# A bank that ScalarE seeds: the first of seven products is copied into the accumulator of the fourth, and VectorE's sum of the two goes

## The reference, cut to what matters

```python
def _L0_ffn_ref(hidden_states, w_gate, w_up, w_down):
    def _bitlinear(x, w):
        scale = jnp.mean(jnp.abs(w))
        q = jnp.round(jnp.clip(w / (scale + EPS), -1.0, 1.0))
        return x @ (q * scale).T
    gate = _bitlinear(hidden_states, w_gate)   # w_gate (2752, 1024)
    up = _bitlinear(hidden_states, w_up)       # w_up   (2752, 1024)
    return _bitlinear(gate * up, w_down)       # w_down (1024, 2752)
x = x + _L0_ffn_ref(_L0_cond_ref(x, cond, ...), w_gate, w_up, w_down)   # x (64, 64, 1024)
```

## Time and profile before

| | |
|---|---|
| median of 3 runs | 1727.45 us (1727.34 to 1729.59) |
| profiled execution, first to last instruction | 1726.1 us; the page gives no other time of it |
| what lies around the span, median less span | 1.35 us |
| TensorE matmuls, busy | 1707.7 us, 12424 instructions |
| VectorE, busy | 1096.0 us, 1786 instructions |
| ScalarE, busy | 575.6 us, 921 instructions |
| granted TensorE clock, mean | 0.999 |

### The profile page before, as it was taken

How to read it: one execution, slowest core, us unless ns; L and a number is a source line. 1 busy time by engine, 2 the same in 40 slices (tenths; PEclk the granted TensorE clock), 3 DMA queues, 4 the chain that set the end, 5 groups by cost and what they waited for, 6 DMA issues and landing times.

```text
span 1726.1 us, 31355 instructions
## 1 busy us (share of the span) xinstructions
PE 1707.7 (99%) x12424; PEld 1215.6 (70%) x12424; DVE 1096.0 (63%) x1786; ACT 575.6 (33%) x921; POOL 28.0 (2%) x59
## 2 busy tenths in 40 slices
PE   6999999999999999999999999999999999999999
PEld 5554545968769596795958768596776959678684
DVE  6898895555766468554685646755576545855464
ACT  6887732312333133230333213231233313323120
POOL 0010000000000000000000000000000000000000
PEclk9999999999999999999999999999999999999999
DMA  8666626312242032420224211331223313132021
GB/s 342 249 229 239 221 96 219 121 44 97 76 148 96 22 108 77 168 66 22 107 102 164 65 75 54 129 137 43 97 76 126 101 40 108 65 124 79 29 87 49
DMA packets 59735, 194.06 MB, mean 112 GB/s; under 512 B 5280, under 2 KB 5600, under 8 KB 59584
## 3 DMA queue, kind: packets, MB, share of 16 engines
q1 hardware_dynamic: 56432, 177.49, 28.9%
q0 software_dynamic: 2560, 14.36, 2.2%
q10 hardware_dynamic: 592, 0.09, 0.0%
HBM read 160.90 MB, written 31.01 MB: 111 GB/s over the span
## 4 chain that ended last, share of the span: by engine, by line
PE 97%; DVE 2%; DMA 1%; issue 0%; ACT 0%; SPq 0%; DVEq 0%
PE ps L881 52%; PE ps L938 25%; PE ps L658 17%; PE ps L899 2%; PE ps L761 1%; DMA xa<-in_x_dram 1%; DVE wsum L1318 0%; DVE ys L1413 0%; DVE msk L1458 0%; DVE ys L1380 0%; DVE xa L1529 0%; DVE prod L1496 0%; DVE yp L1418 0%; ACT wdT L1106 0%; SPq L493 0%
## 5 line engine op out<-in xcount | busy, mean ns | idle before, releaser
L881 PE MATMUL ps<-yp,wgT 128*128 128x256 f16 x4116 | 902.4, 273 | 1.1 <-issue 1.1
L881 PE MATMUL ps<-wuT,wgT 128*128 128x256 f16 x4116 | 902.4, 273 | 0.0
L881 PEld LDWEIGHTS ps<-yp,wgT 128*128 128x128 fp8e4 x4116 | 402.9, 98 | 50.8 <-issue 2.9
L881 PEld LDWEIGHTS ps<-wuT,wgT 128*128 128x128 fp8e4 x4116 | 402.7, 98 | 48.3
L938 PE MATMUL ps<-wdT,inter 128*128 128x512 fp8e4 x1960 | 433.2, 379 | 0.0
L938 PEld LDWEIGHTS ps<-wdT,inter 128*128 128x128 f16 x1960 | 191.1, 98 | 227.2 <-issue 1.4
L1762 DVE SCALAR_TENSOR_TENSOR xr<-ps,osc,xr 128x512 f32<-128x512 f32 x210 | 156.4, 748 | 168.2 <-PE ps L938 128.4
L1711 DVE TENSOR_TENSOR wdT<-ps,msk 128x512 f32<-128x512 f32 (+1 forms) x77 | 51.3, 666 | 207.1 <-PE ps L881 207.1
L1241 ACT COPY raw<-ps 128x512 f32<-128x512 f32 (+1 forms) x77 | 43.7, 567 | 314.6 <-PE ps L881 314.0
L1248 ACT COPY msk<-ps 128x512 f32<-128x512 f32 (+1 forms) x77 | 43.6, 567 | 138.1 <-PE ps L881 138.1
L1263 ACT COPY inter<-ps 128x256 f32<-128x256 f32 x70 | 26.1, 372 | 180.1 <-PE ps L881 180.1
(11 more groups left out here) (229 smaller groups left out, 1497.9 us busy)
## 6 DMA issues: line engine op xcount, KB each, us to landing
wgT<-wcomb SPq DMA_DIRECT2D x70, 896.0 KB, 4.7
wdT<-dcomb SPq DMA_DIRECT2D x14, 2240.0 KB, 10.9
xa<-in_x_dram SPq DMA_DIRECT2D x8, 2048.0 KB, 7.8
out_dram<-xr SPq DMA_DIRECT2D x64, 256.0 KB, 2.0
wcomb<-xa POOLq DMA_DIRECT2D x17, 448.0 KB, 3.0
xr<-in_L_ffn_w_down_dram SPq DMA_DIRECT2D x9, 512.0 KB, 5.5
inter<-in_L_ffn_w_gate_dram SPq DMA_DIRECT2D x7, 512.0 KB, 16.6
wdT<-in_L_ffn_w_up_dram SPq DMA_DIRECT2D x7, 512.0 KB, 4.4
```

Of the source, the lines that this page charges most:

```text
L881: last = nc.tensor.matmul(out, w, operand(i, OPERAND[what])[:, k, :], start=(start and h + k + i == 0), stop=(k == KQ - 1 and i == 1), ski ...
```

## The change

P2 gets no first-matmul flag any more: ScalarE's `copy_p1` copies P1 from `PB` straight into `PA` (ps4), and P2 accumulates on it, so that `PA` holds P1 + P2. VectorE's `c11` is gone. A new ScalarE copy, `gate11`, brings the gate half of `PA` to SBUF (`g11`, half of the old `t1`), and `i11` takes its up half from PSUM. P2 now waits for `s_t1`, and `copy_p1` for `s_i11` of the pair before (pairs 0 and 6: for the outputs that still read ps4). TensorE's order is P1, P4 of the pair before, P2; in pair 0, which has no P4 before it, the first half of P5 (8 matmuls) stands between P1 and P2, and its second half stays where P5 was.

```diff
-                first, start = isinstance(c, int) and c == FIRST, what in ("P1", "P2", "P5")
+                first, start = isinstance(c, int) and c == FIRST, what in ("P1", "P5")
...
-                elif what == "P2":
-                    if p == 0:
-                        pe.wait_ge(s_o, done - 1)
...
-                    else:
-                        pe.wait_ge(s_c11, n)
-                elif what == "P6":
+                elif what in ("P2", "P6"):
                     pe.wait_ge(s_t1, n + 1)
...
                     product(c, p, "P1")
-                    product(c, p, "P2")
                     if p:
                         product(c, p - 1, "P4")
+                    else:
+                        product(c, p, "P5", 0)
+                    product(c, p, "P2")
                     if more and p - 2 in range(KH):
                         conv(c + 1, p - 2)
                     product(c, p, "P6")
-                    product(c, p, "P5")
+                    product(c, p, "P5", None if p else 1)
...
             def copy_p1(c, p):
                 n, w = NS * (c - FIRST) + p, width(p)
                 act.wait_ge(s_m1, n + 1)
...
+                    act.wait_ge(s_i11, NPR * (c - FIRST) + p)
+                nc.scalar.copy(PA[:, 0:w], PB[p % 2][:, 0:w]).then_inc(s_t1, 1)
+
+            def gate11(c, p):
+                act.wait_ge(s_m2, NS * (c - FIRST) + p + 1)
+                if p == NPR:
+                    act.wait_ge(s_i21, NS * (c - FIRST) + NPR)
+                elif p:
+                    act.wait_ge(s_i11, NPR * (c - FIRST) + p)
+                nc.scalar.copy(g11 if p < NPR else g21, PA[:, 0:HALF]).then_inc(s_g11, 1)
...
                     if p:
                         gate21(c, p - 1)
+                    gate11(c, p)
                     copy_p16(c, p)
...
-                V.tensor_tensor(rr if p < NPR else g21, PA[:, 0:w], t1[:, 0:w], ALU.add).then_inc(s_c11, 1)
-
             def i11(c, p):
-                dve.wait_ge(s_c11, NS * (c - FIRST) + p + 1)
+                dve.wait_ge(s_g11, NS * (c - FIRST) + p + 1)
...
-                V.scalar_tensor_tensor(a_block(p, A11), rr[:, u], PROD, rr[:, g], ALU.mult, ALU.mult).then_inc(s_i11, 1)
+                V.scalar_tensor_tensor(a_block(p, A11), PA[:, u], PROD, g11, ALU.mult, ALU.mult).then_inc(s_i11, 1)
```

More of the change, by code:

```diff
@@ L347, in quarter @@
             return ys[:, k:k + KQ, t:t + HALF]
-        t1, q67 = (raw5[:, i * TOK:(i + 1) * TOK] for i in range(2))
+        g11, q67 = raw5[:, 0:HALF], raw5[:, TOK:2 * TOK]
         q6 = [msk_flat.bitcast(f32)[:, i * TOK:(i + 1) * TOK] for i in range(2)]
@@ L454, in adaln_ternary_ffn @@
         s_t1 = sem("s_t1")
+        s_g11 = sem("s_g11")
         s_q6 = sem("s_q6")
         s_q67 = sem("s_q67")
-        s_c11 = sem("s_c11")
         s_c22 = sem("s_c22")
@@ L831, in down, with product @@
                 last.then_inc(s_dn, 1)
-            def product(c, p, what):
+            def product(c, p, what, half=None):
                 n = NS * (c - FIRST) + p
                 done = DN * FIRST + ND2 * (c - FIRST)
-                first, start = isinstance(c, int) and c == FIRST, what in ("P1", "P2", "P5")
+                first, start = isinstance(c, int) and c == FIRST, what in ("P1", "P5")
                 bank = PA if what == "P2" else (PC if what in ("P5", "P3") else PB)[p % 2]
-                if what == "P1":
+                if half == 1:
+                    pass
+                elif what == "P1":
                     pe.wait_ge(s_ring[p % RING], 16 * ((4, 4, 3)[p % RING] * (c - FIRST) + p // RING + 1))
@@ L850, in product @@
                         pe.wait_ge(s_i21, n - 1)
-                elif what == "P2":
-                    if p == 0:
-                        pe.wait_ge(s_o, done - 1)
-                    elif p == GRP + 1:
-                        pe.wait_ge(s_o, done + DOWN[0].index(("P2", 1)) + 1)
-                    else:
-                        pe.wait_ge(s_c11, n)
-                elif what == "P6":
+                elif what in ("P2", "P6"):
                     pe.wait_ge(s_t1, n + 1)
@@ L872, in product @@
                     pe.wait_ge(s_c22, n + 1)
-                if p == 0:
+                if p == 0 and half != 1:
                     pe.wait_ge(s_ylo, KH * c + OPERAND[what] + 1)
-                waited(c)
-                for h in range(2 if p < NPR else 1):
+                if half != 1:
+                    waited(c)
+                for h in range(2 if p < NPR else 1) if half is None else (half,):
                     out = bank[:, h * HALF:(h + 1) * HALF]
@@ L883, in product @@
                                                     skip_group_check=True)
-                last.then_inc(s_done[what], 1)
+                if half != 0:
+                    last.then_inc(s_done[what], 1)
             def rest(c):
@@ L915, in down_group @@
                     elif what == "P1" and j:
-                        pe.wait_ge(s_c11, n + (NS if g else GRP + 1))
+                        pe.wait_ge(s_g11, n + (NS if g else GRP + 1))
+                        pe.wait_ge(s_i11, NPR * (c - FIRST) + (NPR if g else GRP + 1))
                     elif what == "P5" and g == 0:
@@ L1235, in copy_p1 @@
                 act.wait_ge(s_m1, n + 1)
-                if p or not (isinstance(c, int) and c == FIRST):
-                    act.wait_ge(s_c11, n)
-                else:
-                    for i in range(2):
-                        act.wait_ge(s_wst[i], 16 * ((NCB + 1 - i) // 2))
-                nc.scalar.copy(t1[:, 0:w], PB[p % 2][:, 0:w]).then_inc(s_t1, 1)
+                if p == 0:
+                    act.wait_ge(s_o, DN * FIRST + ND2 * (c - FIRST) - 1)
+                    if isinstance(c, int) and c == FIRST:
+                        for i in range(2):
+                            act.wait_ge(s_wst[i], 16 * ((NCB + 1 - i) // 2))
+                elif p == GRP + 1:
+                    act.wait_ge(s_o, DN * FIRST + ND2 * (c - FIRST) + DOWN[0].index(("P2", 1)) + 1)
+                else:
+                    act.wait_ge(s_i11, NPR * (c - FIRST) + p)
[7 more added lines that the diff above has]
+                nc.scalar.copy(g11 if p < NPR else g21, PA[:, 0:HALF]).then_inc(s_g11, 1)
             def copy_p16(c, p):
@@ L1694, in c22 @@
                     dve.wait_ge(s_i12, NPR * (c - FIRST) + p)
-                else:
-                    dve.wait_ge(s_i11, NPR * (c - FIRST) + 1)
+                elif later(c):
+                    dve.wait_ge(s_last, c - FIRST)
                 V.tensor_tensor(rr[:, TOK - w:TOK], PC[p % 2][:, 0:w], q67[:, 0:w], ALU.add).then_inc(s_c22, 1)
@@ L1706, in c12 @@
                 dve.wait_ge(s_q6, n + 1)
[L1707 to L1710, removed]
+                if p < NPR:
+                    dve.wait_ge(s_i22, NPR * (c - FIRST) + p + 1)
                 V.tensor_tensor(rr[:, 0:w], PC[p % 2][:, 0:w], q6[p % 2][:, 0:w], ALU.add).then_inc(s_c12, 1)
@@ L1779, in tail @@
                 dve.wait_ge(s_c12, NS * (c - FIRST) + NS)
+                dve.wait_ge(s_g11, NS * (c - FIRST) + NS)
                 V.scalar_tensor_tensor(blocks4[0][:, 0:HALF], rr[:, g], PROD, g21, ALU.mult, ALU.mult).then_inc(s_last, 1)
@@ L1819, in pairs @@
                     if p < NPR:
-                        c11(c, p)
                         i11(c, p)
@@ L1824, in pairs @@
                         sums3(c, p - 1)
-                    if p == NPR:
-                        c11(c, p)
                     if more and p - 2 in range(KH):
```

## The result

| | before | changed |
|---|---|---|
| median | 1728.03 us (17 runs, 1727.31 to 1729.74) | 1731.02 us (17 runs, 1730.48 to 1733.04) |
| ratio | | 1.0018, 95% interval 1.0011 to 1.0025 |
| profiled span | 1726.1 us | 1728.7 us |

The changed kernel is slower by 3 us. The interval lies above 1 and on both sides of 1.002.

What follows compares the result with a forecast made beforehand. TensorE was taken to bound the kernel, busy 1707.7 of 1726.1 us. Added waits of 2.1 + 1.1 + 0.2 = 3.4 us on the median of 1727.45 gave some 1730.9 us, with an 8 in 10 range of 1728.2 to 1734.2.

Steps and rivals of the forecast that it cites:

- TensorE bounds the kernel, and what VectorE is relieved of is worth 0: TensorE busy 1707.7 of 1726.1 us; removing 77 VectorE sums, some 51 us, gains 0 on the path.
- Three waits a chunk, at P4(9), P2(0) and P7(0): TensorE waits for ScalarE's copies: P4(9) 0.33 us in the loop, 0.24 outside; P2(0) and P7(0) 0.08 each; chance 0.72.
- Their sum, 3.4 us: Over seven chunks: 2.1 us at P4(9), 1.1 in pair 0, 0.2 for register instructions in the loop.
- the first weight load, 0.10, is no longer hidden: At each late wait of TensorE, the exposed first weight load adds 0.10 us to the price.
- I take 0.02: Register instruction between wait and matmul of pair 0 in the loop: 0.02 us, ten times, 0.2 us; upper end 0.3 each.
- a delay after ScalarE's end that is not 0.16: Sign of being wrong: from copy's end to matmul other than 0.16 us (0.06 to the weight load, 0.10 for it).
- The copy ends 0.17 after the start that it has to serve: Pair 10, chunk 2: copy_p167(9) ends at 655.11, P4(9) would start at 654.94; bare lateness 0.17 us.
- The copy into PSUM takes 0.59: ScalarE's copy of P1 into PSUM takes 0.59 us, with 0.45 and 1.05 as ends.
- the waits did not stay hidden: Rival 1: TensorE's queue absorbs weight load and release, the change costs under 1 us, 1727.5 to 1728.5; chance 0.09.
- The write to PSUM was not slow: Rival 2: the copy takes 1.05 us, P2(0) 0.46 later in seven chunks, 3.2 us more, 1734.1; chance 0.09.
- The clock did not fall: Rival 3: TensorE's granted clock falls once a chunk, 7 x 1.7 = 12 us, 1743; chance 0.04.
- Faster did not come: Rival 4: the changed loop body hides the 1.1 us of issue at the loop's way back, 1726.4; chance 0.03.

Runs made afterwards that it cites:

- vector_sum_back: Changed kernel with an unused 128x512 sum on VectorE ahead of each i11, as long as the one taken out; ratio to before 1.0020.
- the last pair of kernels: Chunks 2 to 6 written out without loops: the change with its three waits covered, and the kernel before; medians 1726.77 and 1726.76 us.
- all_cover: Changed kernel with TensorE's products reordered in pairs 10 and 0, and gate11(0) behind copy_p16(0), to give all three waits more cover; ratio to before 1.0001.
- p5_whole_first: Changed kernel with the whole of P5 ahead of P2(0) in pair 0, nothing between P6(0) and P7(0); ratio to before 1.0047.
- ylo_first: Changed kernel with the two waits of a product of pair 0 swapped, s_ylo before ScalarE's copy; ratio to before 1.0009.
- order_alone: Kernel before with only TensorE's new order of products; VectorE's sum, the copy to SBUF and P2's own bank stay; ratio to before 1.0015.
- before_written_out: Kernel before with chunks 2 to 6 written out instead of looped, nothing of the change; median 1726.76 us, ratio to before 0.9990.

## Why the prediction was right, point by point

- *TensorE bounds the kernel, and what VectorE is relieved of is worth 0*: shown by vector_sum_back and by the last pair of kernels.
- *The middle pairs have no wait*: shown: pairs 1 to 9 have no gap in any of the seven chunks, pair 6 behind its down group among them.
- *Three waits a chunk, at P4(9), P2(0) and P7(0)*: shown, and by all_cover that they are the whole loss. In chunks 1 and 7 those of pair 0 did not come: 17 gaps, where the prediction had 21. A loop chunk took 205.75 to 206.14 us from P1(0) to P1(0), where 206.1 was forecast.
- *Their sum, 3.4 us*: 3.34 measured in the gaps, but that it comes so close is luck, since its terms were mis-sized in both directions: P4(9) gave 1.42 us in all where 2.1 was forecast, pair 0 gave 1.92 where 1.3 was. P4(9) was put at 0.33 in the loop and 0.24 outside and was 0.22 and 0.14; the two of pair 0 at 0.08 and 0.02, and were 0.22 and 0.15 in the loop and 0 outside.
  - The term "the first weight load, 0.10, is no longer hidden" failed. p5_whole_first shows 0.01 to 0.03 us from load to matmul. The row that it came from is of fp32 matmuls of 128 columns, where the loads take as long as the matmuls (eight loads from 23.56 on 1.08 us, eight matmuls 1.05).
  - The term "I take 0.02" for the register instruction failed: ylo_first shows 0.10. I had taken it from ScalarE's delay after TensorE, which was no wait behind a register instruction on TensorE. Its stated upper end of 0.3 held. With it fell what the prediction had named as a sign of being wrong, a delay after ScalarE's end that is not 0.16: from the copy's end to the matmul it was 0.24 in pair 0 of the loop, 0.14 at P4(9) in the loop and 0.05 to 0.06 there outside it.
  - Behind it lies a loop term that I did not have. Without a register instruction, too, the load comes 0.11 us after the copy in the loop and 0.05 outside, since in the loop an instruction of its own carries the wait (L777 under ylo_first).
  - "The copy ends 0.17 after the start that it has to serve": 0.08 in the changed kernel's loop (655.51 against 655.43), and 0.17 in order_alone (656.68 + 0.58 = 657.26 against 657.09). The edit changed what c12 on VectorE waits for (i22 of its own pair instead of i11 two pairs on), and with it the instructions of the loop body: c12(8) started 1.46 us ahead of P1(10) before (652.61 and 654.07 in chunk 2) and 1.55 in the changed kernel (653.00 and 654.55). In the changed kernel a register instruction that carried the wait for P3 ahead of this c12 is gone; the kernel before has it in chunk 2 (L1708, ALU_OP, 40 ns, at 652.5). In chunk 7 of the kernel before, written out, there is none either, and c12(8) starts 1.55 us ahead of P1(10) (1672.57 and 1674.12), as in the changed kernel. That agrees with it as the cause; it was not tried alone.
- *The copy into PSUM takes 0.59*: 0.57 (the group's mean is 552 ns with the half-width ones, 567 before). The estimate of 0.57 by the Trainium skill's page "VectorE: DVE Perf Modes" (section "The TRN2 errata — SBUF-src ops pay a fixed extra latency per instruction") is met by this copy, though its table has a row for PSUM to SBUF and none for PSUM to PSUM; the copies from PSUM to SBUF in the same trace take 0.59.
- *Rivals*: the waits did not stay hidden. The write to PSUM was not slow. The clock did not fall: 1.00 in each of seven stretches from 293 to 1728.7 us, one a chunk, in the changed kernel, in order_alone and in p5_whole_first alike. The Trainium skill, "TensorE: Matmul & The Clock Gate", section "A second HAM failure mode: psum-queue depth-cycling", has short idle times between groups of matmuls that make the clock swing; the trace does not agree here, neither with gaps of 0.3 us nor in p5_whole_first with gaps of 1 us, which add up to the stream without any further loss. The 1.2 GHz near 28 us that this rival was priced by came after TensorE had been busy for 1.82 of 4.00 us (24 to 28 us), which is more than the "hardly anything to do" of the prediction. Faster did not come: the way back gave 0.63 us in the profiled execution. What there was to gain at it was put too low, at 1.1 us: before_written_out gains 1.74.
- *The difference of the medians*, 3.0 us, is 0.4 under the sum; the two profiles differ by 2.65 us in the stream: 3.34 of gaps, less 0.63 of the loop's way back (1.74 to 1.11), within 0.1. That the way back is shorter by the change is not shown; in the eight other kernels with the loop it was 0.89 to 1.52. Whether the loss is over or under 0.2% the 17 runs do not settle.

## What to carry to other kernels

Where one engine is full, an order of work is a table of covers: for each wait, what the waiting engine does between the operand's source and the wait, against the price of the way through the other engine, here 0.84 us for a copy of 128x512 and 1.03 in a loop. Edges (the first pair, the half-width last one) have less cover than the middle, and there the change lost all it lost. Such gaps do not show as waits on a page where the records overlap; they show in the starts. And an operation that is taken off an engine with time to spare bought nothing here: VectorE's 55 us less were worth 0.

## What the runs showed of the hardware that I had not expected

- From the end of ScalarE's copy to TensorE's dependent weight load: 0.05 us in written-out code, 0.11 in the loop or where the wait that matters is the second of two, 0.21 in the loop with a register instruction behind it. The step from 0.05 to 0.11 goes with a 51 ns instruction of its own that carries the wait ahead of the load (L777 in the loop, L856 in chunk 1 of ylo_first), and not with the increment that L777 also makes.
- A late weight load of fp8 delays the matmul by 0.01 to 0.03 us, not by its own 0.10.
- The way back of this loop, whose body is a whole chunk, took 0.08 to 0.57 us more than straight code, different each time; with chunks 2 to 6 written out the kernel before gains 1.7 us (1429.10 to 1427.36), more than any part of this change. What makes it differ stays open.
- The copy of 128x512 fp32 from PSUM takes 570 ns into PSUM and 586 ns into SBUF, on average of 70.
